# VectorE transposes the row maxima of an attention step before it gathers keys for the step two ahead

## The reference, cut to what matters

```
xq = round(min(1, |x|) * 7) / 7 ;  x = conv3x3(xq, sign(W) * mean|W|) + b
q, k, v = split(layernorm(x) @ wqkv + bqkv)            # per region: (49, 64, 64)
_, idx = top_k(mean(q) @ mean(k).T, 4)                 # per region: 4 chosen regions
scores = einsum('brqhd,brkhd->brhqk', q, k[idx]) * scale
out = einsum('brhqk,brkhd->brqhd', softmax(scores), v[idx]) @ wo + bo
x = x + out ;  x = x + gelu(layernorm(x) @ w1 + bm1) @ w2 + bm2
```

## Time and profile before

| | |
|---|---|
| median of 3 runs | 5534.44 us (5532.67 to 5543.07) |
| profiled execution | 5529.57 us |
| its span, first to last instruction | 5527.8 us |
| mean granted TensorE clock | 0.921 |
| busy share PE, DVE, ACT, POOL | 84%, 62%, 59%, 50% |
| VectorE's reduces L724 | 1568, 1921.3 us |
| VectorE's key copies L643 | 3136, 623.5 us |
| VectorE's transposes L731 | 1568, 315.1 us |

### The profile page before, as it was taken

One profiled execution on the slowest core, in us unless ns is written; L12 is line 12 of the kernel. 1 busy time (PEld: TensorE's weight loads), 2 busy tenths in 40 slices (PEclk: granted clock), 3 DMA queues, 4 the chain that ended last, 5 costly groups with the idle time before them and its releaser, 6 DMA issues.

```text
span 5527.8 us, 230234 instructions
## 1 busy us (share of the span) xinstructions
PE 4665.2 (84%) x68754; PEld 3201.2 (58%) x68754; DVE 3450.3 (62%) x7969; ACT 3268.0 (59%) x6282; POOL 2749.0 (50%) x9656
## 2 busy tenths in 40 slices
PE   2388888988889888888988888888888888888888
PEld 1265565656556565565656656565565656556564
DVE  2266666666666666666666666666665666667665
ACT  1156656565565656656565665756566565565657
POOL 1245455454554645555454554545455464554553
PEclk9589998998999999999998999999998998999989
DMA  1333333333423333243333423333343333423311
GB/s 53 101 91 99 80 108 81 95 84 92 107 68 102 81 95 100 75 109 83 97 87 91 108 69 105 84 102 93 83 111 73 97 83 92 109 74 104 87 38 33
DMA packets 627125, 487.33 MB, mean 88 GB/s; under 512 B 483793, under 2 KB 613969, under 8 KB 615537
## 3 DMA queue, kind: packets, MB, share of 16 engines
q10 hardware_dynamic: 335360, 205.62, 16.6%
q1 hardware_dynamic: 290416, 265.73, 16.4%
HBM read 262.38 MB, written 208.73 MB: 85 GB/s over the span
## 4 chain that ended last, share of the span: by engine, by line
PE 46%; DMA 16%; issue 10%; ACT 7%; SPq 7%; DVE 6%; DVEq 4%; ACTq 3%; POOL 1%; POOLq 0%
DMA max_d<-tr 12%; PE ps L988 10%; PE ps L1002 8%; PE ps L1019 7%; PE ps L881 5%; PE ps L938 3%; DMA xin<-in_x 3%; DVE mx L724 3%; DVEq L223 3%; ACTq L237 2%; ACT pt L832 2%; ACT hid L813 2%; PE ps L901 2%; PE ps L949 2%; SPq L327 2%
## 5 line engine op out<-in xcount | busy, mean ns | idle before, releaser
L724 DVE TENSOR_REDUCE mx<-ps 128x4 f32<-128x1024 f32 x1568 | 1921.3, 1225 | 1631.0 <-PE ps L988 1238.6
L832 ACT ACTIVATE pt<-ps 128x512 f32<-128x512 f32 x3136 | 1694.5, 592 | 769.5 <-PE ps L1002 646.7
L506 POOL COPY vg<-vs 64x64 f32 x6272 | 1529.6, 244 | 782.0 <-POOL kg L490 576.7
L490 POOL CAST kg<-ks 96x128 fp32r x3136 | 853.2, 297 | 1488.4 <-PE ps L1002 1142.2
L988 PE MATMUL ps<-kg,qm 96*128 96x256 f32 x6272 | 1324.6, 335 | 290.9 <-DVE mx L724 149.6
L988 PEld LDWEIGHTS ps<-kg,qm 96*128 96x128 f32 x6272 | 933.1, 199 | 944.1 <-issue 808.6
L1002 PE MATMUL ps<-qm,kg 97*128 97x256 f32 x6272 | 1138.8, 303 | 207.7 <-ACT pt L832 148.0
L1002 PEld LDWEIGHTS ps<-qm,kg 97*128 97x128 f32 x6272 | 926.7, 202 | 302.0 <-ACT pt L832 218.5
L1019 PE MATMUL ps<-pt,vg 128*32 128x64 f32 x50176 | 1089.2, 231 | 0.0
L1019 PEld LDWEIGHTS ps<-pt,vg 128*32 128x32 f32 x50176 | 825.2, 115 | 224.5 <-issue 34.7
L643 DVE CAST kg<-ks 96x128 fp32r x3136 | 623.5, 241 | 119.5 <-issue 114.9
(11 more groups left out here) (109 smaller groups left out, 3941.6 us busy)
## 6 DMA issues: line engine op xcount, KB each, us to landing
qk_d<-stg SPq DMA_DIRECT2D x224, 448.0 KB
qm<-qk_d ACTq DMA_DIRECT2D x1792, 42.0 KB
ks<-qk_d ACTq DMA_DIRECT2D x96, 784.0 KB, 6.2
vs<-v_d ACTq DMA_DIRECT2D x64, 784.0 KB, 7.0
xin<-in_x SPq DMA_DIRECT2D x119, 224.0 KB
xi_d<-xi SPq DMA_DIRECT2D x112, 224.0 KB
qk_d<-stg SPq DMA_DIRECT2D x112, 224.0 KB
max_d<-tr SPq DMA_DIRECT2D x1568, 2.0 KB
```

The costliest lines, as they stand in the source:

```text
L490: j = pool.tensor_copy(kg[slot][0:NP3, :, 2 + k, :], ks[place(m)[0]][0:NP3, :, bass.ds(region, 1), :].rearrange("p g o t -> p g (o t)"))
L506: j = pool.tensor_copy(dst.rearrange("p j (e x) -> p j e x", e=2)[:, :, :, 0:HD], vs[place(m)[0]][rows, bass.ds(region, 1), :].rearrange(" ...
L724: v.tensor_reduce(mx[h % 2][:].rearrange("p (g j e) -> p g j e", g=2, j=2)[:, :, :, 0], ps[:, 0:2, :].rearrange("p g (j k) -> p g j k", j= ...
L832: act.activation(pt[m % 2][:, c], ps[:, 2 + c, :], ACT.Exp, scale=float(HD) ** -0.5).then_inc(S["pt_ready"], 1)
```

## The change

In VectorE's step the transpose, with its wait for the reduce, is moved ahead of `keys`. Nothing is added and nothing taken away.

```
--- before
+++ after
@@ step(p, h, kind) of VectorE
                     v.tensor_reduce(mx[h % 2]..., ps[:, 0:2, :]..., AX.X, ALU.max).then_inc(S["mx_ready"], 1)
-                if live(h + AHEAD, kind):
-                    keys(p, h + AHEAD, kind)
                 if live(h, kind):
                     v.wait_ge(S["mx_ready"], T + 1)
                     settled(v)
                     v.transpose(tr[h % 2][:], mx[h % 2][:]).then_inc(S["tr_ready"], 1)
+                if live(h + AHEAD, kind):
+                    keys(p, h + AHEAD, kind)
                 if kind == "loop":
                     strip_ahead(p + 1, h)
                     route(p + 1, h)
```

## The result

The changed kernel takes 6089.73 us (median of 4 runs, 6084.27 to 6092.62) against 5538.75 us of the kernel before, run beside it: a ratio of 1.0992, 95% interval 1.0972 to 1.1012, or 551 us more. The forecast was 5825 us with a range up to 6010. The direction and the root of the loss were right; the sum was not, and one of its terms above all.

What follows compares the result with a forecast made beforehand. TensorE, busy 84%, was taken as the engine to keep fed, with VectorE's longer step making it late: 176 + 60 + 78 - 21 = 293 us on 5529.57 gives 5823, say 5825 us; range 5640 to 6010.

Steps and rivals of the forecast that it cites:

- The cover of the load: VectorE's step: the reduce hides the region-number load today; with the wait first, cover is gone in all 1568 steps.
- The rival by that page's rule for engine instructions: VectorE's sequencer: load stays under the reduce, slack swallows the change, time stays 5529 us; chance 5%.
- VectorE's step grows by 1.0 us: Each VectorE step: next operation can start 2.55 us after the reduce instead of 1.54; bounds zero and 2.0 us.
- Finishing strips, 176 us: 112 finishing strips: L974 starts 1.8 us later in five of a pair's seven, 1.0 in two; ends 112 and 202 us.
- 78 us for the clock: TensorE in finishing strips: longer idle before L974 brings 1.2 GHz stretches, 0.7 us for each of 112; ends zero and 190.
- Preparation strips, 60 us: 105 preparation strips: VectorE becomes the limit in two of a pair's seven, 0.2 us each for others; ends nothing and 147.
- The gain of the earlier hop, 21 us: First hop of the maxima: starts 0.1 us sooner for 208 reduces that waited for it, 21 us taken off.
- The third rival: Lateness spreads: VectorE binds every preparation strip (147 us), finishing strips pay 392 us with the clock; 6069 us, chance 11%.

Runs made afterwards that it cites:

- run 1: Changed kernel with the load of region numbers put ahead of the wait for the reduce, transpose still ahead of the copies: 5591.86 us, ratio 1.0123.
- run 2: Kernel before with only a wait for VectorE's reduce added ahead of the gather, transpose still behind the gather: 6208.83 us, ratio 1.1242.
- run 10: Changed kernel with constants in place of the region numbers, so without the load on VectorE: 5569.41 us, ratio 1.0086.
- run 4: Kernel before with the change made only outside steps 18 to 59 of a loop pass, in those with finishing strips: 5838.61 us, ratio 1.0571.
- run 7: Changed kernel with idle TensorE time filled by unread matmuls, eight ahead of L974's wait, five ahead of the scores in preparation strips: 5963.44 us, ratio 1.0796.
- run 5: Changed kernel with the whole gather moved to the end of VectorE's step, behind the strips' operations: 5742.79 us, ratio 1.0391.
- run 3: Kernel before with the change made only in steps 18 to 59 of a loop pass, preparation strips alone: 5798.14 us, ratio 1.0498.
- run 6: Changed kernel with the load ahead of the wait for the reduce and the gather's copies last, behind the strips' operations: 5540.33 us, ratio 1.0032.
- run 9: Changed kernel with SyncE's stores of a preparation strip issued one step later, offsets 8 to 10 instead of 7 to 10: 6075.86 us, ratio 1.1006.
- run 11: Kernel before with five unread filling matmuls ahead of L974's wait: 5552.5 us, ratio 1.004.

## Why the prediction was wrong, by its own steps

- **The cover of the load: right.** Runs 1, 2 and 10 show it from three sides. The Trainium skill (Perfetto Trace Analysis, sequencer-only instructions) says that the sequencer fetches its next instruction only after such a wait has been met; the trace agrees, with the load 0.2 us behind the transpose. The rival by that page's rule for engine instructions falls with it, since this wait has the other form.
- **VectorE's step grows by 1.0 us: right in quiet steps.** The next reduce can start 2.63 us after the last, forecast 2.55. The step that failed here is the choice of the median for the load: "It is far nearer the median, which 1.0 rests on". Rows 4 had the maximum of 1.546 us; what the sum lacked is that the mean of all 1568 records was 0.60 us and that the long ones gather in one kind of strip. With the change two steps of six have loads of 1.46 and 0.82 us on average, which is 0.93 + 0.29 = 1.2 us a strip. That holds for six strips of a pair's seven (the stores of the last one fall into step 62 and later): some 110 us over 15 pairs. In the kernel before, the loads were nearly as long (1.28 us at offsets 3 and 9), under the reduce for the most part.
- **Finishing strips, 176 us and 78 us for the clock: about right.** The trace gives 267 us and 31 in the last pair, run 4 gives 317. L974's wait came out at 307.5 us; the forecast was near 300. Run 7 took back 86 us here (222.9 less 217.2 us, 15 times), close to the 78 of the clock. The cover that the clock's term counted on is there too: TensorE's wait for ScalarE ahead of L1002 fell from 148.0 to 27.2 us with the change and is 110.9 in run 7. That the late hand-over carries the rest is likely from L974's wait and run 5, but no run changes it alone.
- **Preparation strips, 60 us: wrong, 264 us in the trace and 276 us in run 3.** This is the step that failed, and two things in it. VectorE's demand was put at 18.4 us a strip; with 2.63 us a step, the operations and, in six strips of seven, the long loads it is 6 x 2.63 + 3.1 + 1.2 = 20.1 us (18.9 in the seventh). And the sentence "The others last longer already, waiting for a hop, or for ScalarE while it issues DMAs; I give them 0.2 each" held for none of them: a pair's seven strips lasted 16.8 to 19.5 us before and 19.4 to 21.8 with the change, and each of them grew, by 0.8 us at least. So VectorE became the limit in nearly all of them: its idle time ahead of the reduces in these steps fell from 508 to 110 us over the 15 pairs, and TensorE's wait for the reduce ahead of L988 grew there from 81 to 232 us.
- **How the 264 us divide, as an estimate.** A pair's demand by the figures above, 139.5 us, against the 125.8 of before gives 13.7 x 15 = 205 us. Run 7 puts 42 us on the clock (143.4 less 140.6 us, 15 times). Some 17 us stay open, and since VectorE still waits a little in these steps, the 205 are an upper figure.
- **The clock: right in kind, short by a place.** The prediction looked for the lower level only behind L974. The preparation strips have it too: 438 us of their time over the 15 pairs are at 1.2 GHz, against 142 before. TensorE's timeline there:

```profile
2533.82 0.71 PE L988 MATMUL ps<-kg,qm 96*128 96x256 f32 x4 [1.80 <-DVE mx L724]
...
2536.22 1.86 PE L897 MATMUL ps<-xh,wqk 64*128 64x448 f32 x4 [0.63 <-DVE xh L653]
2538.10 1.19 PE L988 MATMUL ps<-kg,qm 96*128 96x256 f32 x4
```

```profile
2538.00:2541.00 3.00, 2.99 (x42) 2.62 (x40) 1.97 (x5) 1.88 (x4) 0.49 (x2) 0.50 0.10 20
```

Behind waits of 1.80 and 0.63 us for VectorE the granted clock is 0.50 (1.2 GHz), and the scores take 1.19 us instead of 0.71.
- **The gain of the earlier hop, 21 us: not seen.** Run 6, which has the early transpose and a covered load, is 0.3% slower than before; its steps are longer for another reason, so whether the hop by itself gives anything stays open.
- **The third rival**, lateness that spreads to every preparation strip and a full price of the clock, gave 6069 us and had 11%. Its condition, that VectorE binds every preparation strip, is nearly what came. That its total lies close to the measured 6089.73 us is luck: it had 147 us for the preparation strips and 392 for the finishing ones, and the trace shows 264 and some 300 with the last pair.

## What to carry to other kernels

A wait that an engine's sequencer itself executes stops everything behind it in that list, also the scalar work that would have run under the instruction waited for; before moving a wait forward, list what the sequencer did under that cover. Idle time found as a share of the span is no cushion: compare the new length of the engine's step with each kind of stretch, all of them, and with the durations as they are in that stretch. And an engine that makes TensorE wait a little longer may pay twice, since the granted clock falls behind such waits.

## What the runs showed of the hardware that was not expected

VectorE's load of two region numbers from SBUF into registers took 0.53 us with the DMA engines at 0.42 and 0.31 of their time, and 1.49 and 1.65 us with the DMA engines full (1.02 and 1.05). Run 9 moved the long loads by moving SyncE's stores; what in these stores slows the load is not shown. A wait on VectorE's own last result, placed where it orders nothing new, cost 12% (run 2). Matmuls whose results nobody reads took some 116 us off a kernel with waits of some 3 us ahead of L974 (run 7), and made one with waits of 1.2 us 0.4% slower (run 11).
